# A two-layer attention and mixture-of-experts kernel: the FFN down projection with activations as the stationary operand

## The reference, cut to what matters

```python
def body(acc, ws):                       # layer 0: 32 experts of 176 units, 8 of them chosen per token
    wg, wu, wd, cw = ws
    h = jax.nn.silu(x @ wg.T) * (x @ wu.T)
    return (acc + cw[:, None] * (h @ wd.T), None)
shared = jax.nn.silu(x @ sWg.T) * (x @ sWu.T) @ sWd.T
...
x = x + jnp.tanh(g_ffn[0]) * _L0_ffn_ref(_layernorm(x, axis=-1), ...)
```

## Time and profile before

| | |
|---|---|
| median of 3 runs | 1071.76 us (1071.3 to 1072.67) |
| span of the profiled execution, first to last instruction | 1068.4 us |
| mean granted TensorE clock in it | 0.953 of 2.4 GHz |
| TensorE busy, matmuls | 936.1 us, 88% |
| VectorE, ScalarE, GpSimd busy | 675.6, 565.0, 363.6 us |
| FFN 0, first gate matmul to last down matmul | 327.7 to 734.7 us |
| FFN 1, the same | 835.3 to 1062.1 us |

### The profile page before, as it was taken

How to read it: one execution, slowest core, us unless ns; L and a number is a source line. 1 busy time by engine, 2 the same in 40 slices (tenths; PEclk the granted TensorE clock), 3 DMA queues, 4 the chain that set the end, 5 groups by cost and what they waited for, 6 DMA issues and landing times. The chain is left out here.

```text
span 1068.4 us, 17409 instructions
## 1 busy us (share of the span) xinstructions
PE 936.1 (88%) x5931; PEld 709.5 (66%) x5972; DVE 675.6 (63%) x1119; ACT 565.0 (53%) x1014; POOL 363.6 (34%) x359
## 2 busy tenths in 40 slices
PE   5547888888879699999999999995897899999998
PEld 5544445444567588888888888884454678888886
DVE  6988999999965544454454544545786535445454
ACT  5538999999966233333333333333677533333432
POOL 3515666666646222222222222213322712222220
PEclk9869999999979799999999999998799889999999
DMA  5001000000001111111111111011550211111101
GB/s 176 2 1 61 1 1 0 0 0 0 1 16 45 30 45 48 55 44 44 44 48 55 44 44 44 29 60 48 170 165 14 59 45 45 44 44 46 43 1 40
DMA packets 27494, 45.41 MB, mean 43 GB/s; under 512 B 3392, under 2 KB 17600, under 8 KB 27456
## 3 DMA queue, kind: packets, MB, share of 16 engines
q1 hardware_dynamic: 27184, 44.40, 13.6%
q10 hardware_dynamic: 272, 0.52, 0.1%
HBM read 39.67 MB, written 5.24 MB: 42 GB/s over the span
## 5 line engine op out<-in xcount | busy, mean ns | idle before, releaser
L894 POOL TENSOR_TENSOR wlo<-wraw,whi 128x768 fp32r<-128x768 f32 x73 | 134.6, 1846 | 432.0 <-ACT whi L935 432.0
L979 DVE TENSOR_TENSOR kstack<-psum,comb_p 128x512 f32<-128x512 f32 x136 | 94.1, 692 | 284.6 <-PE psum L220 284.6
L218 PE MATMUL psum<-actT_hi,whi 128*128 128x512 f32 x584 | 234.0, 401 | 2.2 <-ACT comb_p L940 2.2
L220 PE MATMUL psum<-actT_hi,wlo 128*128 128x512 f32 x584 | 232.9, 399 | 0.0
L219 PE MATMUL psum<-actT_lo,whi 128*128 128x512 f32 x584 | 232.6, 398 | 0.0
L946 ACT ACTIVATE kstack<-psum 128x512 f32<-128x512 f32 x146 | 87.2, 597 | 201.4 <-PE psum L220 201.4
L739 POOL TENSOR_SCALAR p<-e 128x1024 f16<-128x1024 f32 x128 | 133.7, 1044 | 80.4 <-ACT e L660 40.2
L698 DVE TENSOR_REDUCE nmax<-psum 128x1 f32<-128x1024 f32 x128 | 156.3, 1221 | 7.0 <-PE psum L594 5.5
L953 ACT ACTIVATE h_hi<-kstack 128x512 fp32r<-128x512 f32 x146 | 91.7, 628 | 128.8 <-DVE kstack L984 122.1
L660 ACT ACTIVATE e<-psum,nmax 128x1024 f32<-128x1024 f32 x128 | 142.4, 1113 | 4.1 <-DVE nmax L698 2.7
L218 PEld LDWEIGHTS psum<-actT_hi,whi 128*128 128x128 f32 x584 | 111.1, 190 | 29.1 <-ACT comb_p L940 2.9
(11 more groups left out here) (189 smaller groups left out, 1182.0 us busy)
## 6 DMA issues: line engine op xcount, KB each, us to landing
wraw<-in_wffn SPq DMA_DIRECT2D x73, 384.0 KB, 3.0
parts_dram<-h_hi SPq DMA_DIRECT2D x8, 512.0 KB, 3.3
actT_hi<-parts_dram SPq DMA_DIRECT2D x24, 128.0 KB, 3.1
actT_lo<-parts_dram SPq DMA_DIRECT2D x24, 128.0 KB, 3.0
ctxT<-in_ctxT SPq DMA_DIRECT2D x2, 512.0 KB, 5.0
x<-in_x SPq DMA_DIRECT2D x1, 1024.0 KB, 8.3
ctok<-in_ctx SPq DMA_DIRECT2D x1, 1024.0 KB, 10.6
out<-x SPq DMA_DIRECT2D x4, 256.0 KB, 2.4
```

Of the source, the lines that this page charges most:

```text
L218: pe.matmul(out, l_hi, r_hi, start=start, stop=False, **kw)
L220: return pe.matmul(out, l_lo, r_hi, start=False, stop=stop, **kw)
L894: pool.tensor_tensor(wlo[:, i, :], wraw[:, i, :], whi[:, i, :].bitcast(F32), ALU.subtract).then_inc(c["w_lo"], 1)
L979: dve.tensor_tensor(u_c[:, cut], bank(6 + n), comb_p[:, cut], ALU.mult).then_inc(c["uc"], 1)
```

## The change

The two operands of the down projection change places. The h parts of 128 tokens become stationary and the down weights (256 output features) move. A bank of PSUM holds two groups of 128 tokens by 256 features, tokens on partitions, as x has them. So the copies into `yT` and the transposes go, and VectorE adds bank q to x as soon as its own six last matmuls are done. Line numbers of the changed file are one lower at 218 to 1015 (218 becomes 217).

```diff
-                    for n, cut in halves():
+                    w_hi, w_lo = whi[:, i, 2 * D:3 * D], wlo[:, i, 2 * D:3 * D]
+                    for n, _ in halves():
                         pe.wait_ge(c["h_lo"], j * NH + n + 1)
-                        for k in range(KD):
-                            at = 2 * D + k * P
-                            last = mm3(pe, bank(2 * k + n), whi[:, i, at:at + P], wlo[:, i, at:at + P],
-                                       h_hi[:, i % 2, cut], h_lo[:, i % 2, cut], start=first, stop=final,
-                                       skip_group_check=True)
-                        if final:
-                            last.then_inc(after["y"], 1)
+                        for t in range(n * (NT // NH), (n + 1) * (NT // NH)):
+                            out = bank(t // 2)[:, t % 2 * D:(t % 2 + 1) * D]
+                            rows = slice(t * P, (t + 1) * P)
+                            hi, lo = h_hi[:, i % 2, rows], h_lo[:, i % 2, rows]
+                            pe.matmul(out, hi, w_hi, start=first and t % 2 == 0, stop=False, skip_group_check=True)
+                            pe.matmul(out, hi, w_lo, start=False, stop=False, skip_group_check=True)
+                            last = pe.matmul(out, lo, w_hi, start=False, stop=final, skip_group_check=True)
+                            if final and t % 2 == 1:
+                                last.then_inc(after["y"], 1)
...
         def expert_sum(name):
-            def on_act(act):
-                for n in range(NH):
-                    act.wait_ge(c["y"], n + 1)
-                    act.activation(yT[:, 0, n * BANK:(n + 1) * BANK], bank(n), ACT.Copy).then_inc(c["y_a"], 1)
             def on_dve(dve, gate, norm):
-                for n in range(NH):
-                    dve.wait_ge(c["y"], n + 1)
-                    dve.tensor_copy(yT[:, 1, n * BANK:(n + 1) * BANK], bank(2 + n)).then_inc(c["y_d"], 1)
                 for q in range(NT // 2):
-                    dve.wait_ge(c["t_ps"], q + 1)
-                    dve.scalar_tensor_tensor(x[:, 2 * q:2 * q + 2, :], bank(4 + q).rearrange("p (t n) -> p t n", t=2),
+                    dve.wait_ge(c["y"], q + 1)
+                    dve.scalar_tensor_tensor(x[:, 2 * q:2 * q + 2, :], bank(q).rearrange("p (t n) -> p t n", t=2),
...
-            def on_pe(pe):
-                for q in range(NT // 2):
-                    pe.wait_ge(c["y_a"], q // NH + 1)
-                    pe.wait_ge(c["y_d"], q // NH + 1)
-                    ...  (four transposes of yT into bank 4 + q)
...
-            pool.wait_ge(c5["y"], NH)
+            pool.wait_ge(c5["y"], NT // 2)
```

More of the change, by code:

```diff
@@ L181, in build @@
         h_f = view("k", T)
-        yT = view("k", KD * T).rearrange("p (k t) -> p k t", k=KD)
         route_sb = view("k", T)
@@ L1083, in expert_sum @@
         def expert_sum(name):
-            c = {n: sem(f"{name}_{n}") for n in ("y", "y_a", "y_d", "t_ps", "x")}
-            def on_act(act):
-                for n in range(NH):
-                    act.wait_ge(c["y"], n + 1)
-                    act.activation(yT[:, 0, n * BANK:(n + 1) * BANK], bank(n), ACT.Copy).then_inc(c["y_a"], 1)
+            c = {n: sem(f"{name}_{n}") for n in ("y", "x")}
             def on_dve(dve, gate, norm):
-                for n in range(NH):
-                    dve.wait_ge(c["y"], n + 1)
-                    dve.tensor_copy(yT[:, 1, n * BANK:(n + 1) * BANK], bank(2 + n)).then_inc(c["y_d"], 1)
                 for q in range(NT // 2):
-                    dve.wait_ge(c["t_ps"], q + 1)
-                    dve.scalar_tensor_tensor(x[:, 2 * q:2 * q + 2, :], bank(4 + q).rearrange("p (t n) -> p t n", t=2),
+                    dve.wait_ge(c["y"], q + 1)
+                    dve.scalar_tensor_tensor(x[:, 2 * q:2 * q + 2, :], bank(q).rearrange("p (t n) -> p t n", t=2),
                                              tgate[:, gate:gate + 1], x[:, 2 * q:2 * q + 2, :],
@@ L1105, in on_dve @@
                         norm(q)
-            def on_pe(pe):
-                for q in range(NT // 2):
-                    pe.wait_ge(c["y_a"], q // NH + 1)
-                    pe.wait_ge(c["y_d"], q // NH + 1)
[L1112 to L1116, removed]
-                    last.then_inc(c["t_ps"], 1)
-            return c, on_act, on_dve, on_pe
+            return c, on_dve
         c3 = {n: sem("c3_" + n) for n in ("o_ps", "o_hi", "o_lo", "y_ps", "x")}
@@ L1154, in build @@
         SCALE1 = HD1 ** -0.5
-        c5, sum_act, sum_dve, sum_pe = expert_sum("s0")
+        c5, sum_dve = expert_sum("s0")
         c6 = {n: sem("c6_" + n) for n in ("dve", "pool", "stats", "rstd", "xn", "staged", "scores", "max", "bias", "exp",
@@ L1260, in attend1_act @@
         def attend1_act(act):
-            sum_act(act)
             for u in range(NT // 2):
@@ L1330, in attend1_pe @@
         def attend1_pe(pe):
-            sum_pe(pe)
             def scores(turn, u):
@@ L1386, in build @@
                  "y": c5["y"]})
-        c8, sum1_act, sum1_dve, sum1_pe = expert_sum("s1")
+        c8, sum1_dve = expert_sum("s1")
         stored = sem("stored")
@@ L1400, in build @@
             ffn(block, 1, "f1", None,
-                {"sp": store, "pool": lambda pool: None, "act": sum1_act, "dve": lambda dve: sum1_dve(dve, 3, None),
-                 "pe": sum1_pe, "y": c8["y"]})
+                {"sp": store, "pool": lambda pool: None, "act": lambda act: None,
+                 "dve": lambda dve: sum1_dve(dve, 3, None), "pe": lambda pe: None, "y": c8["y"]})
 def _columns(w):
```

## The result

The change makes the kernel slower: 1075.32 us (median of 5 runs, 1074.3 to 1076.63) against 1071.84 (5 runs, 1071.3 to 1072.67), ratio 1.0038 [1.0025, 1.005]. A second comparison, with 17 runs of the kernel before, gave 1.0036 [1.0023, 1.0049]. The profiled execution took 1076.63 us, the longest of its five, with a span of 1074.8 us. One later execution of the kernel before took 1202.22 us at a granted clock of 0.757; no time or ratio in this document contains it.

A forecast was written before the change was run, and what follows sets the result against it. Inside the FFNs the time was taken as the sum of TensorE's matmul prices. Down part +7.4, end -2.57 and attention start -0.28 make +4.6 us on 1071.76, so 1076.4 us, range 1071.5 to 1081.0.

The forecast's parts named there:

- The down part: FFN tile loops: 24 matmuls of 256 columns at 119.4 ns replace 12 of 512, on 70 tiles; +7.4 us.
- The end: Kernel's end: three of four additions to x hide under matmuls, the last ends 0.78 us after the last matmul; -2.57 us.
- The start of the attention: From FFN 0 to the attention: GpSimd's first norm instruction stops waiting for VectorE; -0.28 us, bounds 0 and 0.36.
- The half clock: Stretches at clock 0.50, such as after FFN 1's routing wait: nothing added, taken as 0, possibly +-1.5 us.
- sign of being wrong: Half-clock stretches differing by more than 3 us in length would show the forecast wrong.
- Around the span: Outside the profiled span: the 3.4 us by which the runs' median stands above it stay, since the launch is the same.
- A: Down part: 256-column matmuls keep its favour over gate and up, 117.5 to 118 ns; about 1073.5 us, no net change; chance 0.17.
- B: Down part: matmuls at the transposes' 109 ns, 1059 us; counts all down to half price, below 1069.6 us; chance 0.06.
- C: Down part: denser loads collide with FFN traffic, 122.4 ns per matmul, +12.4 us, 1081.4 us; chance 0.12.
- D: Down part: loads not hidden at all, 5.4 us per tile, +183 us, about 1252 us; chance 0.01.

The follow-up runs named there:

- runs with half tiles: The change with 64 of each 128 tokens stationary, or with 128 of the 256 down-weight columns moving: 1063.79 us and 1061.58 us, one run each.
- turned wide kernel: The changed kernel with 12 down matmuls of 512 moving gate and up columns, four of eight token groups: 1067.28 us against 1071.86 before, ratio 0.9965.
- narrow, not turned: The kernel before with each 512-column down matmul split into two of 256, weights still stationary: 1077.04 us against 1071.86, ratio 1.0054.
- the change again: The changed kernel, unaltered, measured once more beside the kernel before: 1074.21 us against 1071.07, ratio 1.0036.
- ends alone: The kernel before without the copies and 16 transposes at each FFN's end, down matmuls kept: 1067.85 us against 1071.86, ratio 0.9962.
- down part alone: The kernel before with the down projection turned as in the change, copies and transposes kept: 1078.06 us against 1071.86, ratio 1.0058.
- turned at the end alone: The kernel before with only FFN 1's last two down parts turned, earlier sums transposed back and mostly lost: 1069.44 us against 1071.07, ratio 0.9987.
- turned in FFN 1 alone: FFN 0 as in the kernel before, FFN 1 and the kernel's end as in the change: 1071.18 us against 1071.41, ratio 0.9999.
- turned at the end, sums kept: FFN 1's last two down parts turned, only a bank's first transpose opening the accumulation, against the kernel before: 1070.47 us against 1071.7, ratio 0.9991.
- the kernel before again: The kernel before, unchanged, as one of the kernels compared: 1071.25 us against 1071.41, ratio 1.0004.

## Why the prediction was right

It said 1076.4 us, slower, by 4.6; it is 1075.3, slower by 3.5 (3.1 in the second set).

- *The down part.* Predicted 70 x 0.106 = +7.4 us; the FFN stages grew by 8.77, less twice the 0.11 us that belongs behind them 8.55. The sign and the path were right, the size was 13% short. A tile grew by 8.48 - 8.36 = 0.12 us and not by 0.106 (the row gave 119.4 ns, the FFN 119.9, and the old price was rounded up), which makes 70 x 0.12 = 8.4. The rest is the wait for the routing in FFN 0: the prediction took the two down parts before it as covered, but they are 0.24 us longer and the wait shrank only from 7.49 to 7.38, so some 0.13 us of them was paid.
- *The reason for the term.* The prediction took a row and did not say why halves cost more than half. The runs with half tiles show it: a near tie between the load (109 ns) and the matmul (114 ns). All of the 8.4 us is that: 24 x 70 x (119.9 - 113.8) = 10.2 us, less 1.8 for the halves being, without it, slightly cheaper than half of 229.7.
- *The end.* Predicted -2.57 and three hidden additions, the last 0.78 us behind the last matmul; found -2.76 and 0.78. The additions take 0.73 us each instead of 0.68, but three of them are hidden all the same. The span ends 2.98 us after the last addition before (1068.39 - 1065.41) and 2.80 after (1074.81 - 1072.01); the prediction had taken the store behind it as equal, and that is its 0.2 us.
- *The start of the attention.* Predicted -0.28, found -0.33 in the first pair of profiles, with GpSimd's wait gone as predicted. The second profile of the change has 0.24 us less yet. Over all fourteen profiles, counted from the end of the last down matmul, the kernels without the copies start 0.3 to 1.1 us sooner. So the first pair's agreement to 0.05 us is luck, and the bound of 0.36 was too narrow for most pairs.
- *The half clock.* Taken as 0 +- 1.5. The windows from the first score matmul to FFN 1, and the first 12 us of them, of the kernel before:

```profile
749.12:835.25 86.13, 72.99 (x349) 41.52 (x349) 62.30 (x188) 58.95 (x176) 24.74 (x48) 0.88 0.40 116
...
749.12:761.12 12.00, 9.91 (x37) 6.25 (x38) 7.94 (x23) 6.56 (x23) 3.48 (x7) 0.58 0.80 232
```

  and of the kernel after:

```profile
756.33:841.44 85.11, 71.59 (x348) 40.72 (x349) 62.43 (x188) 59.06 (x176) 24.68 (x48) 0.89 0.39 114
...
756.33:768.33 12.00, 10.06 (x40) 6.05 (x40) 8.72 (x26) 7.30 (x25) 3.46 (x7) 0.65 0.77 227
```

  The same work is 1.0 us shorter after, with TensorE 1.4 us less busy, and the granted clock tells where: 0.65 against 0.58 over the first 12 us, while in the 12 us behind them it is 1.00 in both. The clock comes back sooner after the score matmuls begin. All six profiles with 24 matmuls to a down part in FFN 0 have 84.6 to 85.3 us for this stage, seven of the eight others 85.6 to 86.6; the turned wide kernel, with 84.4, is the exception. The length of FFN 0 is not the cause: two of the six are the runs with half tiles, whose FFN 0 is shorter than before (405.3 and 402.6 us) and which have 85.2 and 84.8. The cause is not shown. Over a whole execution the effect is larger, as the table at the end of this part shows: about 6 us less time at half clock in the second set, beyond the 3 us that the prediction had named as a sign of being wrong.
- *Around the span.* The prediction took 3.4 us. It is 1.8; the rest was one quick execution. It did no harm, because the same number stood on both sides.
- *The range.* It was given as holding both the clock's +-1.5 us and 0.0 to +8.4 us. Together these make 1070.3 to 1081.7, wider than the 1071.5 to 1081.0 stated; the result lies in either.
- *The rivals.* Cheaper halves (A, at most 118 ns) and half price (B) are excluded by 119.9 ns. But the reason given against A was wrong: the down part's favour of 3 ns does not come from h moving, since the turned wide kernel keeps it (2.76 us) with h stationary. A fails because 256 columns with a full load cost more than half, not because the favour is lost; what the favour comes from is open. Colliding loads (C) had the right idea, that it is the loads, and the wrong place: the projections pay nearly the same. The argument that little else works beside the projections misread the rows, however. In the output projection's window VectorE is busy for 4.39 of 5.00 us, GpSimd for 3.50, and the DMA share is 0.24; in the FFN it is 162 and 72 of 333 us, and 0.15. What speaks against C is that the distance hardly follows the traffic: 118.6 ns in the Q projection, where the DMA share is 0.00 (window below), 119.4 in the output projection, 119.9 in the FFN. D, loads that are not hidden, is excluded: it needed 5.4 us for a down part.

```profile
35.70:39.20 3.50, 3.50 (x32) 3.50 (x30) 2.37 (x5) 1.91 (x1) 1.96 (x2) 1.00 0.00 0
```

  The Trainium skill's sentence that a load overlaps only with a matmul on other rows of the array (TensorE: Matmul & The Clock Gate, "The mechanism") doesn't hold for these full-height loads; the text above it in that section also names the background weight buffer as a case in which a load runs ahead, and the 2.88 us of a down part agree with that. An estimate by the Trainium skill's price of a load (same page, "LDWEIGHTS (loading the stationary operand)"), 107 ns for 128 columns, agrees with the 109.4 ns found where the matmul is the shorter one.

**Times against stages.** The touched parts sum to +5.5 us, the times say +3.1 to +3.5, and other runs miss the sum of their touched stages too. The granted clocks on record go with these gaps. With the mean granted clock c of an execution, TensorE's clock is halved for 2 x (1 - c) of its span. That is coarse for one execution (0.001 of the clock is 2.1 us), so the table has means over 5 to 21 executions. At half clock a 256-column matmul takes 0.21 us, against 0.12, so a microsecond less at half clock saves at most about half a microsecond.

| run | time at half clock, less than before (us) | worth at most | time below the sum of the touched stages |
|---|---|---|---|
| narrow, not turned | 8.5 | 4.2 | 3.3 |
| the change again | 5.9 | 2.9 | 2.0 |
| ends alone | 4.6 | 2.3 | 1.7 |
| down part alone | 4.5 | 2.2 | 2.6 |
| turned, wide | 3.8 | 1.9 | 1.5 |
| turned at the end alone | 2.9 | 1.4 | 0.9 |
| turned in FFN 1 alone | 2.6 | 1.3 | 0.5 |
| turned at the end, sums kept | 2.1 | 1.0 | 0.5 |
| the kernel before again | -0.6 | -0.3 | 0.2 |

The stages are those of the run's own profile. The two columns on the right go together, in size and, but for the down part alone, in order. So most of the missing time is, as far as this shows, time at full instead of half clock outside the touched stages; single profiles with their 2.4 us of scatter can't place it. The mean granted clock was 0.9546 for the change in the second set and 0.9517 for the kernel beside it. Why one kernel gets more of the full clock than another is not shown.

So the closeness of 1076.4 to 1075.3 is in part luck. The prediction's mechanism, a dearer matmul in every tile against two shorter ends, is what the runs show; but its sum was some 0.9 us below what the touched stages measured (+5.5), and the half clock, which it put at nothing, goes with the 2 us by which the time lies below them.

## What to carry to other kernels

When an operand exchange halves the moving columns, price it by the trace's own matmuls of the new shape: here a full-height load of 128 fp32 columns costs 109 ns, so 512 columns hide it (230 ns), and 256 columns nearly tie with it and pay 6 ns each, times every matmul in the loop. A gain that happens once (2.8 us at the end) has to be set against a loss in each turn of a loop (0.12 us, 70 times). Where only the end gains, turn only the end: that kept the 2.8 us at 2.1 us of extra work, a net gain of 0.8 us by the stages and 1.2 by the times, at the edge of what they can tell. A sum of stages from one profile should also be held against the granted clocks of several executions before a difference of 2 us is believed.

## What the runs showed of the hardware

- A load of 128 fp32 columns (109.4 ns beside a short matmul) and a matmul of 256 (113.8 ns beside a short load) need nearly the same time and cost 119.9 together, more than either; beside 512 columns (230 ns) the load costs nothing.
- The listed duration of a load (190 ns for 128 columns, 130 for 64) is not its price: with 128 moving columns, loads of 190 ns follow each other every 109 ns.
- Matmuls of 512 columns cost about 230 ns in the down part, in either orientation, and about 233.5 in gate and up.
- The kernel before runs nearly always at one of two mean granted clocks: 59 of 73 executions at 0.951 take 1071.7 us on average, 13 at 0.953 or 0.954 take 1069.7.
- A profile differs from the next of the same kernel by up to 2.4 us in the first attention alone, and by 0.03 us in an FFN bound by TensorE: a difference of 1 us in the FFN can be read from one profile, in the attention it can't.
